# Expert stage of a conv/attention hybrid: token tiles of 112 become 128, chunks of 224 become 256, one-hot rows get a pitch of 66 elements

## The reference

```
x_norm = x * inv * norm_w
q = (x_norm @ wq).reshape(B, T, HEADS, 2, DIM_KEY)           # 8 heads, 2 halves, 32
sim = jnp.einsum('bthpd,hkpd->pbthk', q, keys)               # 64 keys a head and half
s1, i1 = jax.lax.top_k(sim[0], K)                            # K = 16
s2, i2 = jax.lax.top_k(sim[1], K)
all_idx = i1[..., :, None] * NUM_KEYS + i2[..., None, :]
all_scores = s1[..., :, None] + s2[..., None, :]
final_scores, pk = jax.lax.top_k(all_scores, K)
final_idx = jnp.take_along_axis(all_idx, pk, axis=-1)
hidden = gelu(x_norm . expert_down[final_idx]) * relu(final_scores)
out = sum over heads and K of hidden * expert_up[final_idx]  # 4096 experts
```

## Time and profile before

| what | value |
|---|---|
| time, median of 3 runs | 2684.61 us (2683.7 to 2685.41) |
| time of the profiled execution | 2689.78 us |
| span of the profiled execution | 2688.1 us |
| PE busy | 2236.6 us, 83% |
| DVE busy | 1847.0 us, 69% |
| ACT busy | 663.9 us, 25% |
| POOL busy | 435.8 us, 16% |
| mean granted TensorE clock | 0.82 |

### The profile page before, as it was taken

The page is one execution under the profiler, slowest core; times in us unless marked ns, Lnnn a source line. Parts: engine busy times, 40 slices in busy tenths (PEclk is TensorE's granted clock), DMA queues, the critical chain, the costliest instruction groups (busy, mean ns, idle before and its releaser), DMA issues. The chain is left out here.

```text
span 2688.1 us, 50156 instructions
## 1 busy us (share of the span) xinstructions
PE 2236.6 (83%) x18017; PEld 1940.0 (72%) x18017; DVE 1847.0 (69%) x7732; ACT 663.9 (25%) x1527; POOL 435.8 (16%) x521
## 2 busy tenths in 40 slices
PE   6585999955989889989989889989888799648994
PEld 3464788734889788888989889889888577326663
DVE  4334666448889889898898898898895577440003
ACT  1432455432211111211211211111111255402220
POOL 2003444310101201102102012012012310030003
PEclk8777999966788697787787887887786799869996
DMA  1104444225000000000000000000000233042323
GB/s 53 34 18 98 106 108 99 47 73 118 5 4 1 5 5 2 5 5 2 5 1 5 5 1 5 5 1 5 1 1 1 65 83 81 7 165 82 104 92 102
DMA packets 87043, 107.85 MB, mean 40 GB/s; under 512 B 26222, under 2 KB 75502, under 8 KB 86062
## 3 DMA queue, kind: packets, MB, share of 16 engines
q1 hardware_dynamic: 81328, 96.62, 13.7%
q0 software_dynamic: 3296, 6.43, 0.9%
q10 hardware_dynamic: 2176, 1.61, 0.2%
HBM read 70.61 MB, written 30.51 MB: 38 GB/s over the span
## 5 line engine op out<-in xcount | busy, mean ns | idle before, releaser
L1540 PE MATMUL peer_x_ps<-peer_oh_h,peer_oh_a 128*128 128x32 bf16 x3136 | 417.2, 249 | 6.1 <-DVE peer_oh_l L1812 4.4
L1540 PEld LDWEIGHTS peer_x_ps<-peer_oh_h,peer_oh_a 128*128 128x128 bf16 x3136 | 414.2, 149 | 8.5 <-DVE peer_oh_l L1812 5.7
L1541 PE MATMUL peer_x_ps<-peer_oh_l,peer_oh_a 128*128 128x32 bf16 x3136 | 417.8, 249 | 0.0
L1541 PEld LDWEIGHTS peer_x_ps<-peer_oh_l,peer_oh_a 128*128 128x128 bf16 x3136 | 412.9, 149 | 3.6 <-issue 1.5
L1516 PE MATMUL peer_x_ps<-peer_xc,peer_dt 128*128 128x224 f32 x1792 | 374.4, 373 | 31.7 <-DMA peer_up<-in_L_ffn_expert_up_dram 19.4
L1482 POOL TENSOR_TENSOR peer_g<-peer_g,peer_qt 128x448 f32<-128x448 f32 x112 | 189.7, 1715 | 1275.0 <-ACT peer_qt L1639 1274.9
L1550 PE MATMUL peer_out_ps<-peer_g,peer_up 128*128 128x224 f32 x1792 | 370.9, 372 | 30.6 <-issue 28.4
L1516 PEld LDWEIGHTS peer_x_ps<-peer_xc,peer_dt 128*128 128x128 f32 x1792 | 362.1, 204 | 40.0 <-issue 34.6
L1550 PEld LDWEIGHTS peer_out_ps<-peer_g,peer_up 128*128 128x128 f32 x1792 | 361.1, 203 | 37.6 <-issue 32.4
L1617 ACT ACTIVATE peer_g<-peer_x_ps 128x448 f32<-128x448 f32 x224 | 121.9, 544 | 652.1 <-PE peer_x_ps L1516 652.1
L1277 DVE TENSOR_REDUCE l_attn_mx<-l_attn_s_ps 98x4 f32<-98x392 f32 (+1 forms) x320 | 175.0, 560 | 140.4 <-PE l_attn_s_ps L1047 100.6
(11 more groups left out here) (308 smaller groups left out, 3633.5 us busy)
## 6 DMA issues: line engine op xcount, KB each, us to landing
moe_w<-in_L_ffn_w_dram SPq DMA_DIRECT2D x16, 1024.0 KB, 9.1
l_attn_pieces_q_dram<-l_attn_pieces_q SPq DMA_DIRECT2D x16, 294.0 KB, 3.9
l_attn_pieces_k_dram<-l_attn_pieces_k SPq DMA_DIRECT2D x16, 294.0 KB, 3.1
l_attn_stq<-l_attn_pieces_q_dram SPq DMA_DIRECT2D x16, 294.0 KB
l_attn_stk<-l_attn_pieces_k_dram SPq DMA_DIRECT2D x16, 294.0 KB
peer_g<-n_L_ffn_expert_down_dram SPq DMA_DIRECT2D x8, 512.0 KB, 6.7
peer_up<-in_L_ffn_expert_up_dram SPq DMA_DIRECT2D x2, 2048.0 KB
l_xi<-net_x SPq DMA_DIRECT2D x16, 196.0 KB, 2.3
```

Source lines behind the costliest of these rows:

```text
L1540: nc.tensor.matmul(x_ps[q][:, i * J:(i + 1) * J], oh_a[hb % 2][:, :, t], oh_h[hb % 2][:, :, t], start=True, stop=False)
L1541: mm = nc.tensor.matmul(x_ps[q][:, i * J:(i + 1) * J], oh_a[hb % 2][:, :, t], oh_l[hb % 2][:, :, t], start=False, stop=True)
```

## The change

The tile becomes 128 tokens, the chunk 256, the half 64 and the quarter 16. 3136 tokens are then 12 chunks and a rest of 64 tokens, which is a thirteenth chunk with one tile, one half, and 64 columns in its matmuls. So every step gets its number of tokens as an argument (`now`, and `then` for the chunk that follows). The row pitch of the one-hot buffers becomes HP = 66 elements, of which 64 are written and read. What the decoding needs besides `sel`, and the codes themselves, move into the rest of `oh_a` (`behind`). For that the wait of `make_codes` for the end of the last scatter moves from behind the candidates' top 16 to ahead of the candidates. Last, `weigh` no longer stands in one piece behind `one_hots` of the following half: its four quarters stand between the four instructions of it.

```diff
@@ -1361,7 +1361,7 @@
     NH, NK, DK, TOP = 8, 64, 32, 16
     G16 = 2 * NH
     NP = NH * TOP
-    TT = 112
+    TT = 128
     NTILE = 2
     CT = NTILE * TT
     NCHUNK = NT // CT
@@ -1370,7 +1370,10 @@
...
+    HP = HT + 2
     GT = HT // 4
+    REST = NT - NCHUNK * CT
+    assert REST == HT
     LOWEST = -3.4028235e38
 
...
-        oh_a = [S.sb(f"oh_a{p}", [P, P, HT], BF16) for p in range(2)]
-        oh_h = [S.sb(f"oh_h{p}", [P, J, HT], BF16) for p in range(2)]
-        oh_l = [S.sb(f"oh_l{p}", [P, J, HT], BF16) for p in range(2)]
+        oh_a = [S.sb(f"oh_a{p}", [P, P, HP], BF16) for p in range(2)]
+        oh_h = [S.sb(f"oh_h{p}", [P, J, HP], BF16) for p in range(2)]
+        oh_l = [S.sb(f"oh_l{p}", [P, J, HP], BF16) for p in range(2)]
...
-        i16f, step16 = S.sb("i16f", [TT, NTILE * G16, TOP]), S.sb("step16", [TT, 2, TOP, HH], BF16)
         cv = sc[0]
-        f16, p16 = S.sb("f16", [TT, HH, TOP]), S.sb("p16", [TT, HH, TOP], U32)
-        pos_b, col_b = S.sb("pos_b", [TT, PP], BF16), S.sb("col_b", [TT, PP], BF16)
-        t1, t2, t3 = S.sb("t1", [TT, PP]), S.sb("t2", [TT, PP]), S.sb("t3", [TT, PP])
-        bits, col = S.sb("bits", [TT, PP], U32), S.sb("col", [TT, PP], U32)
         starts_b, ranks_b = S.sb("starts_b", [TT, TOP, TOP], BF16), S.sb("ranks_b", [TT, TOP, TOP], BF16)
 
-        sel = [oh_a[p][0:TT, :, :].rearrange("t r k -> t (r k)")[:, 0:TOP * PP].rearrange("t (a k) -> t a k", a=TOP) for p in range(2)]
+        flat = [oh_a[p][0:TT, :, :].rearrange("t r k -> t (r k)") for p in range(2)]
+        sel = [flat[p][:, 0:TOP * PP].rearrange("t (a k) -> t a k", a=TOP) for p in range(2)]
+
+        def behind(p, word, words, dt):
+
+            o = TOP * PP + 2 * word
+            return flat[p][:, o:o + 2 * words].bitcast(dt)
+
+        t1, t2, t3 = (behind(0, i * PP, PP, F32) for i in range(3))
+        bits, col = behind(0, 3 * PP, PP, U32), behind(0, 4 * PP, PP, U32)
+        pos_b, col_b = behind(0, 5 * PP, PP // 2, BF16), behind(0, 5 * PP + PP // 2, PP // 2, BF16)
+        f16 = behind(0, 6 * PP, PP, F32).rearrange("t (h a) -> t h a", a=TOP)
+        p16 = behind(0, 7 * PP, PP, U32).rearrange("t (h a) -> t h a", a=TOP)
+        i16f = behind(1, 0, 2 * PP, F32).rearrange("t (g a) -> t g a", a=TOP)
+        step16 = behind(1, 2 * PP, PP, BF16).rearrange("t (w a h) -> t w a h", w=2, a=TOP)
         i1, i2 = t2, t3
-        codes = S.sb("codes", [TT, 3, PP])
+        codes = behind(1, 3 * PP, 3 * PP, F32).rearrange("t (s k) -> t s k", s=3)
...
             for p in range(2):
-                chunk(p, p, False)
+                chunk(p, p, CT, CT)
             with eng.Fori(1, NCHUNK // 2 - 1) as i:
                 for p in range(2):
-                    chunk(2 * i + p, p, False)
+                    chunk(2 * i + p, p, CT, CT)
             for p in range(2):
-                chunk(NCHUNK - 2 + p, p, p == 1)
+                chunk(NCHUNK - 2 + p, p, CT, CT if p == 0 else REST)
+            chunk(NCHUNK, 0, REST, 0)
...
             steps(sp, NCHUNK // 2 - 1, body)
+            sp.wait_ge(h_done, NPAIR * (NCHUNK - 1))
+            sp.dma_start(xc[0][:, :, 0:REST], xn_dram[:, :, NCHUNK * CT:NT].rearrange("k p t -> p k t")).then_inc(xc_in[0], 16)
...
-            def chunk(n, p, last):
-
-                for hb in range(LATE, NHB):
+            def chunk(n, p, now, then):
+
+                for hb in range(LATE, now // HT):
...
                 o = 0
                 chain.wait()
+                wait(dve, m_done, 4 * NHB * n)
                 for a0, na, nb in CAND:
...
             def one_hots(n, hb):
+
+                def weigh_last(quarter):
+                    if 0 < hb <= LATE:
+                        weigh(n, hb - 1, quarter)
                 q = hb % 2
                 wait(dve, m_done, 16 * n + 4 * (hb - 1))
                 if hb % 2 == 0:
@@ -1804,43 +1830,50 @@
                     return iota_f[:, 0:rows, :].unsqueeze(2).broadcast_to([P, rows, HT // GT, GT])
 
                 def view(m):
-                    return m[:, :, :].rearrange("p r (a b) -> p r a b", b=GT)
+                    return m[:, :, 0:HT].rearrange("p r (a b) -> p r a b", b=GT)
                 nc.vector.tensor_tensor(view(oh_a[q]), spread(a_t, P), number(P), ALU.is_equal)
+                weigh_last(0)
                 chain.step(nc.vector.tensor_tensor(view(oh_l[q]), spread(b_t, J), number(J), ALU.is_equal))
+                weigh_last(1)
                 chain.wait()
-                for dst, wt in ((oh_h, wh_t), (oh_l, wl_t)):
-                    ins = nc.vector.tensor_tensor(dst[q][:, :, :], oh_l[q][:, :, :], wt[:, ts].unsqueeze(1).broadcast_to([P, J, HT]), ALU.mult)
-                ins.then_inc(oh_ready, 1)
-
-            def weigh(n, hb):
-
-                for q in range(4):
-                    dve.wait_ge(m_done, 4 * NHB * n + 4 * hb + q + 1)
-                    ts = slice(hb * HT + q * GT, hb * HT + (q + 1) * GT)
-                    nc.vector.tensor_tensor(g[:, :, ts], g[:, :, ts], x_ps[q][:, 0:GT * J].rearrange("p (t j) -> p j t", j=J),
-                                            ALU.mult).then_inc(g_done, 1)
+                nc.vector.tensor_tensor(oh_h[q][:, :, 0:HT], oh_l[q][:, :, 0:HT], wh_t[:, ts].unsqueeze(1).broadcast_to([P, J, HT]), ALU.mult)
+                weigh_last(2)
+                nc.vector.tensor_tensor(oh_l[q][:, :, 0:HT], oh_l[q][:, :, 0:HT], wl_t[:, ts].unsqueeze(1).broadcast_to([P, J, HT]),
+                                        ALU.mult).then_inc(oh_ready, 1)
+                weigh_last(3)
+
+            def weigh(n, hb, q):
+
+                dve.wait_ge(m_done, 4 * NHB * n + 4 * hb + q + 1)
+                ts = slice(hb * HT + q * GT, hb * HT + (q + 1) * GT)
+                nc.vector.tensor_tensor(g[:, :, ts], g[:, :, ts], x_ps[q][:, 0:GT * J].rearrange("p (t j) -> p j t", j=J),
+                                        ALU.mult).then_inc(g_done, 1)
 
             for t in range(NTILE):
-                top_halves(0, t)
-            make_codes(0)
-
-            def chunk(n, p, last):
-                if p == 0:
+                top_halves(0, t, TT)
+            make_codes(0, tile_rows(CT))
+
+            def chunk(n, p, now, then):
+                if p == 0 and now == CT:
                     chain.turn(n, 2)
-                low_weights(n, 0)
+                tiles, n_hb = tile_rows(now), now // HT
+                low_weights(n, 0, tiles[0])
                 one_hots(n, 0)
-                low_weights(n, 1)
-                for hb in range(NHB - 1):
-                    one_hots(n, hb + 1)
-                    if hb < LATE:
-                        weigh(n, hb)
-                if not last:
-                    for t in range(NTILE):
-                        top_halves(n + 1, t)
-                    make_codes(n + 1)
+                if len(tiles) > 1:
+                    low_weights(n, 1, tiles[1])
+                for hb in range(n_hb):
+                    if hb + 1 < n_hb:
+                        one_hots(n, hb + 1)
+                if n_hb == 1:
+                    for q in range(4):
+                        weigh(n, 0, q)
+                if then > 0:
+                    for t, rows in enumerate(tile_rows(then)):
+                        top_halves(n + 1, t, rows)
+                    make_codes(n + 1, tile_rows(then))
                 dve.wait_ge(out_done, n + 1)
-                xs = x[:, :, bass.ds(n * CT, CT)]
-                nc.vector.tensor_tensor(xs, xs, out_ps[:, 0:KC * CT].rearrange("p (k t) -> p k t", k=KC), ALU.add).then_inc(x_done, 1)
+                xs = x[:, :, bass.ds(n * CT, now)]
+                nc.vector.tensor_tensor(xs, xs, out_ps[:, 0:KC * CT].rearrange("p (k t) -> p k t", k=KC)[:, :, 0:now], ALU.add).then_inc(x_done, 1)
```

More of the change, by code:

```diff
@@ L1575, in _ @@
             pe.wait_ge(w_in, 16 * 4)
-            def chunk(n, p, last):
-                hidden(n, p, range(EARLY))
-                for t in range(NTILE):
-                    turn(n, t)
-                hidden(n, p, range(EARLY, NPAIR))
-                if not last:
-                    queries(n + 1, 1 - p)
-                for hb in range(NHB):
+            def chunk(n, p, now, then):
+                hidden(n, p, range(EARLY), now)
+                for t, rows in enumerate(tile_rows(now)):
+                    turn(n, t, rows)
+                hidden(n, p, range(EARLY, NPAIR), now)
+                if then > 0:
+                    queries(n + 1, 1 - p, then)
+                next_rows = tile_rows(then)
+                for hb in range(now // HT):
                     scatter(n, hb)
-                    if hb < NTILE and not last:
-                        scores(n + 1, hb)
-                experts_out(n)
+                    if hb < len(next_rows):
+                        scores(n + 1, hb, next_rows[hb])
+                experts_out(n, now)
             chunks(pe, chunk)
@@ L1637, in chunk @@
+                for k in range(4 * max(0, now // HT - LATE)):
```

130 lines of the change are left out of this document (66 added, 64 removed).

## The result

The changed kernel takes 2577.72 us (median of 4 runs, 2572.23 to 2580.84), the kernel before 2684.49 us beside it. The ratio is 0.960, 95% interval 0.958 to 0.962, so it is faster by 4.0%. The forecast was 2583 us. Run once more on another occasion, the changed kernel took 2573.47 us against 2682.83, ratio 0.958 (0.956 to 0.961).

A forecast was written before the change was run, and what follows sets the result against it. DVE's share of a DVE-PE loop bounds before; after, both loops come out alike, 107.7 us for 256 tokens. Chunks and rest give -102 us, 2588 profiled, less 5.2 for the median: 2583 us, range 2560 to 2605.

The forecast's parts named there:

- The bound before: Expert stage of the kernel before: DVE's share of a loop through DVE and PE bounds, 103.2 us a chunk.
- the wait's second price: Late hidden part on PE: after a wait for codes it runs partly at the lower clock, about 2.2 us more.
- Tile-wise work as with 112 partitions: DVE's top 16, candidates and decoding: 128 partitions cost the same as 112, 27.7 + 32.3 = 60.0 us.
- Records of 256 columns: f32 matmuls of hidden and out on PE: 217.5 ns a record, +26 ns, +6.7 us a chunk.
- Scatter at 132 bytes: Scatter matmuls on PE: 65.9 ns each with the new pitch too, 6272 of them before and after.
- rival C: Scatter: the 132-byte stride slows TensorE's reads; gain gone at 82 ns, +151 us at 90 ns; chance 0.07.
- One-hots: DVE's one-hot instructions: 4.43 and 1.22 us, +0.9 us a half; a second one stretched while POOL weighs, +1.3 us.
- D: DVE's one-hots lose half their rate because rows no longer touch: +30 us a chunk, 2835 us; chance 0.02.
- Codes just in time: Expert stage: PE's wait for codes falls from 73.9 us to under 15, the late hidden part to 10.4 us.
- Forecast B: Expert stage after the change: DVE's loop stays the bound, 109.3 to 111 us a chunk, about 2610 us; chance 0.28.
- The sum: Expert stage: 11 * 107.7 = 1184.7, twelfth chunk 94.9, rest 36.6; end at 1993.6 instead of 2095.7, -102 us.
- the rest's out: Out product of the last 64 tokens on PE: 128 * 0.12 = 15.4 us, and 1.5 for a cold start.

The follow-up runs named there:

- The cut of 7.9 us on VectorE: The kernel before, with the second eight of the candidates' top 16 left out (the first eight stand twice): 2571.08 us against 2686.51, ratio 0.955.

## Why the prediction was right, step by step

*The bound before.* Right. The cut of 7.9 us on VectorE gave 7.7 in each loop, and ended at TensorE's loop as the forecast had it (95.3, measured 95.4). The 2.2 us for the wait's second price come from one pair of chunks; over all fourteen the late hidden part lay 1.4 us above its 9.26, and the turn some 0.6.

*Tile-wise work as with 112 partitions.* Right: 60.0 us by the forecast and by the timeline after.

*Records of 256 columns.* Forecast 217.5 ns; hidden takes 17.43 / 80 = 218 and 10.5 / 48 = 219 ns. Out was to take 29.3 (25.92 and 128 times 26 ns) and takes 29.5 to 30.7 us.

*Scatter at 132 bytes.* Taken as 65.9 ns, measured 64.6: 8 us less over 6272. That this pitch costs nothing was luck as far as the prediction goes: it had no row of this stride, and rival C, with its threshold at 82 ns, would have come true at a pitch 4 bytes smaller. Its price of 6.3 us for each ns holds roughly (34.9 ns, 204 us of stage, 5.9 us each).

*One-hots.* 4.42 us against a forecast of 4.43; the gap behind the rows costs DVE nothing, so D is wrong. The product beside POOL's is 2.63 us, as before; the second stretched one, for which the forecast added 1.3 us, came in one of the first eleven chunks only (1.23 us in the others). In the twelfth chunk three instructions stretch (2.62, 2.45, 2.51 us) and PE waits 4.29 us for the one-hots. The forecast had nothing there, though the earlier trace rows show one of them stretched in the last chunk before.

*Moved wait, weighing in four places, buffers in `oh_a`.* Nothing, as forecast.

*Codes just in time.* Forecast: wait under 15 us, late hidden 10.4 us; measured 4.8 and 10.5. Forecast B (waits in most chunks, late hidden over 12) did not come, and it was near: VectorE's loop is 105.4 to 105.9 us in ten of eleven chunks, and TensorE's own, without the idle time at the hardware loop's turns, 105.5 to 105.9. The forecast had 107.1 and 107.0, so both stood alike too high; for VectorE's the stretched product that did not come (1.3) and two scatters at 1.3 ns less a matmul (0.3) account for it.

*The sum.* Here the terms are set against the profile, all from turn to turn on PE: start of the stage to the first turn 19.9 forecast and 19.4 measured; eleven chunks 1184.7 and 1175.8 (106.9 each); the twelfth 94.9 and 96.2; the rest 36.6 and 46.2. Sum 1336.1 and 1337.6. So the stage was hit to 1.5 us, but that is luck: two errors cancel, 0.8 us too much in each of eleven chunks, and 10 us too little in the rest. Within the eleven chunks there are two more: the ordinary loop was put at 107.7 us and is 105.8, and some 12 us more, mostly at the hardware loop's three turns, were not in the sum. **The term that failed is the rest's out**, 15.4 + 1.5 us forecast, 27.6 measured. The record's warm price was right (forecast 120 ns, hidden has 113, and the Trainium skill's "TensorE: Matmul & The Clock Gate", LDWEIGHTS, gives 107 for the load of 128 columns by 1.2 GHz, 6% under it). The cold start was not: I took it as 1.5 us, from full chunks, where the clock comes back within the stretch. In the fifth chunk after it is 0.50 in the first 4 us of out and 1.00 from the ninth on. Behind the scatter of the rest (0.53) the short records never got it back.

*The 5 us between forecast and result* lie outside the stage. Ahead of it, in code that is the same, the profiled execution was 8.9 us sooner, behind it 2.6 us shorter; with the stage's 1.5 us the other way that is the 10 us between 2588, the forecast for a profiled execution, and 2577.77. The forecast put the median 5.2 us below a profiled execution, as it was before; here it is the same (2577.72 us), which takes off half of the difference. Over the fourteen profiles of this case the stage begins anywhere from 639.4 to 657.5 us. What of this is scatter of executions and what hangs on the kernel's layout elsewhere isn't settled; of the 112 us of span only 100 to 105 belong to the expert stage.

## What to carry to other kernels

Where two engines close a loop, work out both loops before and after a change: the gain ends where the other loop begins. With both level, as here, taking work off VectorE gave nothing, and taking it off TensorE cost time, since behind the wait that it left the clock was lower. Look, too, for idle time that the wait of before has hidden, such as the one at each turn of a hardware loop. When a tile size changes, look at the byte pitch that it gives to operands read with a stride, the loaded one first; 128 bytes cost half again as much here. Price short stretches of matmul at both clock levels, and try letting the longest dimension move, which saved 10 us in the last 64 tokens.
